# Second gather of a two-layer graph network: a list keyed by block pair and source half, 34 of its groups gathered beside the messages

## The reference

```python
# layer 0, a gated convolution over the edges
z = concat([x[src], x[dst], edge], 1) @ W.T + b
z = (z - mean(z, 0)) * rsqrt(var(z, 0) + 1e-5) * gamma + beta
msg = sigmoid(z[:, :128]) * softplus(z[:, 128:])
x1 = layernorm(x + x + zeros.at[src].add(msg))
# layer 1, on x1
mean1 = segment_sum(x1[src], dst) / max(count(dst), 1)
gain = tanh(norm(x1 - mean1))
h = x1 + 0.2 * (relu(x1 @ W1 + b1) @ W2 + b2) * gain
out = layernorm(x1 + layernorm(h) * gamma1 + beta1)
```

## Time and profile before

| what | us |
| --- | --- |
| median of 3 runs (4361.82 to 4364.86) | 4362.28 |
| the profiled execution, its own time | 4367.02 |
| its span | 4365.3 |
| busy: PE, DVE, ACT, POOL | 3008.4, 2770.6, 2254.1, 2572.3 |

### The profile page before, as it was taken

How to read it: one execution, slowest core, us unless ns; L and a number is a source line. 1 busy time by engine, 2 the same in 40 slices (tenths; PEclk the granted TensorE clock), 3 DMA queues, 4 the chain that set the end, 5 groups by cost and what they waited for, 6 DMA issues and landing times. The chain is left out here.

```text
span 4365.3 us, 81440 instructions
## 1 busy us (share of the span) xinstructions
PE 3008.4 (69%) x17430; PEld 2147.8 (49%) x17431; DVE 2770.6 (63%) x7511; ACT 2254.1 (52%) x6241; POOL 2572.3 (59%) x2618
## 2 busy tenths in 40 slices
PE   6865999899989999999998467666463333333330
PEld 2422444444447777777776366565343333333330
DVE  5798999899975555455554589888534334433337
ACT  2411898899866666666665799999310000000004
POOL 0687777777767777777776000000377777777770
PEclk8998999999999999999999788888665556566665
DMA  6333333333338888888888544443222222222241
GB/s 131 116 94 88 103 102 100 104 102 99 99 104 261 262 260 261 263 260 261 263 262 209 204 181 192 180 180 144 49 52 52 52 52 52 52 52 51 51 48 32
DMA packets 311358, 598.16 MB, mean 137 GB/s; under 512 B 53535, under 2 KB 191944, under 8 KB 305576
## 3 DMA queue, kind: packets, MB, share of 16 engines
q0 software_dynamic: 96992, 228.88, 20.9%
q1 hardware_dynamic: 175480, 246.10, 18.1%
q10 hardware_dynamic: 38736, 121.78, 7.4%
HBM read 406.57 MB, written 189.99 MB: 137 GB/s over the span
## 5 line engine op out<-in xcount | busy, mean ns | idle before, releaser
L346 POOL DMA_INDIRECT rec_d<-arena x830 | 873.0, 1052 | 375.3 <-issue 365.0
L1300 POOL DMA_INDIRECT arena<-x_tab,arena x880 | 847.3, 963 | 315.4 <-issue 277.3
L785 POOL DMA_INDIRECT arena<-b_tab,arena x880 | 838.6, 953 | 302.7 <-issue 262.1
L1332 PE MATMUL psum<-arena 128*128 128x129 f32 x1760 | 410.6, 426 | 694.9 <-DMA arena<-x_tab,arena 635.2
L1332 PEld LDWEIGHTS psum<-arena 128*128 128x128 f32 x1760 | 382.2, 329 | 723.6 <-issue 723.6
L1358 DVE TENSOR_TENSOR arena<-psum,arena 128x129 f32 x880 | 257.7, 293 | 673.3 <-PE psum L1332 553.7
L718 PE MATMUL psum<-arena 128*128 128x440 f16 x3360 | 664.8, 351 | 14.1 <-ACT arena L433 12.9
L806 DVE TENSOR_TENSOR arena<-psum,arena 128x512 f32<-128x512 f32 x440 | 283.6, 686 | 555.7 <-DMA arena<-b_tab,arena 323.2
L898 PE MATMUL psum<-weT,arena 128*128 128x256 f32 x1760 | 548.0, 393 | 58.0 <-DVE arena L806 55.2
L433 ACT ACTIVATE arena<-arena 128x128 f16<-128x128 f16 x1680 | 561.8, 386 | 0.0
L572 DVE TENSOR_SCALAR arena<-iota_t,arena 128x880 f16<-128x880 f16 x840 | 519.3, 663 | 48.4 <-PE psum L718 32.2
(11 more groups left out here) (207 smaller groups left out, 5226.3 us busy)
## 6 DMA issues: line engine op xcount, KB each, us to landing
z_d<-arena ACTq DMA_DIRECT2D x220, 512.0 KB
arena<-z_d SPq DMA_DIRECT2D x44, 2560.0 KB, 8.5
arena<-rec_d SPq DMA_DIRECT2D x220, 260.0 KB
arena<-in_edge_attr SPq DMA_DIRECT2D x83, 640.0 KB
arena<-b_tab,arena POOLq DMA_INDIRECT x880
arena<-x_tab,arena POOLq DMA_INDIRECT x880
rec_d<-arena POOLq DMA_INDIRECT x831, 2.0
b_tab<-arena ACTq DMA_DIRECT2D x49, 128.0 KB, 1.9
```

The lines of the kernel that those rows point to most:

```text
L346: nc.gpsimd.indirect_dma_start(rec_rows, bass.IndirectOffsetOnAxis(e_idx[:, s, k:k + 1], 0), e_buf[:, s, k, :], None).then_inc(s_es[s], 16)
L785: nc.gpsimd.indirect_dma_start(bg[:, s, k, :], None, b_tab, bass.IndirectOffsetOnAxis(rec[:, s, k, H:H + 1].bitcast(I32), 0)).then_inc(s_b ...
L1300: nc.gpsimd.indirect_dma_start(xg[:, s, k, :], None, x1_tab, bass.IndirectOffsetOnAxis(gi[:, s, k:k + 1], 0)).then_inc(s_xg[s], 16)
L1332: last = nc.tensor.matmul(bank(3 * s + q)[:, a * (H + 1):(a + 1) * (H + 1)], hotg[:, s, k, :], xg[:, s, k, :], start=True, stop=True)
```

## The change

- The `dst` list is keyed by 50 numbers in place of 49: the pair of destination blocks (`dst >> 8`, 25 pairs), plus 25 where the source is not in the first 16 blocks. Tiles whose sources all lie in the first 16 blocks come first. `l1_loc` now has 256 values.
- After 16 chunks of the messages DVE stops to normalise the 16 first blocks of `agg` (`normalise_early`), with a root by Newton steps in place of ACT's. SP stores them behind the rows of `x1_tab`. Two conditions on the counts (the first 16 blocks end at or before tile 300; the first 25 keys hold at least 272 tiles) are computed on the chip in `early_enough`; if one fails, POOL waits for the whole table. For the inputs of the reference the counts are 276 and 284, worked out from its edge list.
- POOL then gathers 34 groups of 8 tiles beside the messages and stores each to DRAM (`early_d`).
- The first normalisation moves into the block of the messages. DVE clears `agg1` in POOL's place.
- At the start of the messages SP writes zeros to all of `x1_tab`.
- In the second gather PE and DVE work in rounds of six groups, two early ones (SP loads them from `early_d`) and four gathered; then 8 gathered ones. Each tile has one-hots of 256 columns, two products and an add of 258 columns into a pair of blocks.

The diff, cut to its core:

```diff
-SLOTS = -(-((N_EDGES + BLOCKS * (P - 1)) // P) // (2 * G)) * (2 * G)
+SLOTS = -(-((N_EDGES + 2 * -(-BLOCKS // 2) * P) // P) // (2 * G)) * (2 * G)
+EARLY, EARLY_BLOCKS, EARLY_TILES = 34, 16, 300
+PAIRS = -(-BLOCKS // 2)
+KEYS = 2 * PAIRS
...
-                key(hi_d, dst_i)
+                after(nc.vector.tensor_scalar(t_int, dst_i, 8, None, ALU.logical_shift_right))
+                after(nc.vector.tensor_scalar(v_a, src_i, float(EARLY_BLOCKS * P), float(PAIRS), ALU.is_ge, ALU.mult))
+                after(nc.vector.tensor_tensor(hi_d, t_int, v_a, ALU.add))
...
+                def early_enough():
+                    after(nc.vector.tensor_scalar(early_key, tend[:, PAIRS - 1:PAIRS], float(G * EARLY), None, ALU.is_ge))
+                    after(nc.vector.tensor_tensor(early_src, early_src, early_key, ALU.mult))
+                    after(nc.vector.tensor_scalar(early_key, early_src, float(ROWS), None, ALU.mult))
+                    nc.vector.tensor_scalar(need[:], early_src, -32.0, 48.0, ALU.mult, ALU.add)
...
+        PAUSE = EARLY_TILES // (CG * YG) // CS + 1
...
+            @block.sync
+                def store_early():
+                    sp.wait_ge(s_blank, 16)
+                    sp.wait_ge(s_x1e, 1)
+                    sp.dma_start(x1_tab[ROWS:ROWS + EARLY_BLOCKS * P, :].rearrange("(b p) f -> p b f", p=P), x1e).then_inc(s_xs, 16)
+                sp.wait_ge(s_eps, 2)
+                sp.dma_start(x1_tab[0:ROWS, :].rearrange("(b p) f -> p b f", p=P), no_row.unsqueeze(1).broadcast_to([P, BLOCKS, H + 1])).then_inc(s_blank, 16)
-                chunks(sp, load)
+                chunks(sp, load, store_early, CS - 1)
...
+            @block.gpsimd
+                ready = nc.gpsimd.value_load(need[0:1, 0:1], min_val=16, max_val=48)
+                pool.wait_ge(s_xs, ready)
+                def keep(g):
+                    pool.wait_ge(s_xe[g % 2], (g // 2 + 1) * (16 * G))
+                    pool.dma_start(early_d[:, g, :], xe[:, g % 2, :, :].rearrange("p k f -> p (k f)")).then_inc(s_be[g % 2], 16)
+                for g in range(EARLY):
+                    if g >= 2:
+                        pool.wait_ge(s_be[g % 2], g // 2 * 16)
+                    for k in range(G):
+                        nc.gpsimd.indirect_dma_start(xe[:, g % 2, k, :], None, x1_tab,
+                                                     bass.IndirectOffsetOnAxis(l1_idx[:, g * G + k:g * G + k + 1], 0)).then_inc(s_xe[g % 2], 16)
+                    if g >= 1:
+                        keep(g - 1)
+                keep(EARLY - 1)
...
+                def normalise_early():
+                    dve.wait_ge(s_fl, EARLY_TILES // YG + 2)
+                    for b in range(EARLY_BLOCKS):
+                        last = nc.vector.bn_stats(six[:, b, :], agg[:, b, :])
+                    early(last)
+                    for b in range(EARLY_BLOCKS):
+                        last = nc.vector.bn_aggr(two[:, b, :], six[:, b, :])
+                    early(last)
+                    early(nc.vector.tensor_scalar(ve, two[:, :, 1:2].rearrange("p b a -> p (b a)"), LN_EPS, None, ALU.add))
+                    early(nc.vector.tensor_scalar(re.bitcast(I32), ve.bitcast(I32), 1, None, ALU.logical_shift_right))
+                    early(nc.vector.tensor_scalar(re.bitcast(I32), re.bitcast(I32), -1.0, float(0x5f3759df), ALU.mult, ALU.add))
+                    for _ in range(4):
+                        early(nc.vector.tensor_tensor(te, re, re, ALU.mult))
+                        early(nc.vector.tensor_tensor(te, te, ve, ALU.mult))
+                        early(nc.vector.tensor_scalar(te, te, -0.5, 1.5, ALU.mult, ALU.add))
+                        early(nc.vector.tensor_tensor(re, re, te, ALU.mult))
+                    nc.vector.memset(x1e[:, :, H:H + 1], 1.0)
+                    for b in range(EARLY_BLOCKS):
+                        last = nc.vector.tensor_scalar(x1e[:, b, 0:H], agg[:, b, :], two[:, b, 0:1], re[:, b:b + 1], ALU.subtract, ALU.mult)
+                    last.then_inc(s_x1e, 1)
-                chunks(dve, step)
+                chunks(dve, step, normalise_early)
...
+            def round_of(i):
+                order = (("early", 2 * i, 0, i + 1), ("direct", 4 * i, 0, 2 * i + 1), ("direct", 4 * i + 1, 1, 2 * i + 1),
+                         ("early", 2 * i + 1, 1, i + 1), ("direct", 4 * i + 2, 0, 2 * i + 2), ("direct", 4 * i + 3, 1, 2 * i + 2))
...
+                def product(u, place, kind, n, s, use):
+                    for k in range(G):
+                        wait(pe, s_fg, 8 * u + (k + 2 - RING))
+                        for h in range(2):
+                            last = nc.tensor.matmul(bank((8 * place + k) % RING)[:, h * (H + 1):(h + 1) * (H + 1)], hotg[:, place % 2, k, h * P:(h + 1) * P],
+                                                    rows[:, s, k, :], start=True, stop=True)
                         last.then_inc(s_sg, 1)
...
+                        last = nc.vector.tensor_scalar(hotg[:, place % 2, k, :], iota256[:], l1_loc[:, bass.ds(t, 1)], None, ALU.is_equal)
...
+                        dest = agg1.rearrange("p (c h) f -> p c (h f)", h=2)[:, bass.ds(pairs[k], 1), :].rearrange("p a f -> p (a f)")
+                        nc.vector.tensor_tensor(dest, bank((8 * place + k) % RING)[:, 0:2 * (H + 1)], dest, ALU.add).then_inc(s_fg, 1)
```

More of the change, by code:

```diff
@@ L479, in block_tiles @@
[L479 to L485 removed]
+                    n = offs.shape[1]
@@ L939, in build, with chunks @@
                              "message_transposed", "message_copied", "segment_product", "segment_added", "zero_weights"))
-        def chunks(eng, step):
+        PAUSE = EARLY_TILES // (CG * YG) // CS + 1
+        assert EARLY_TILES == (PAUSE * CS - 1) * CG * YG
+        def chunks(eng, step, pause=None, after_steps=0):
             for c in range(CS):
                 step(c, c, 0)
-            with eng.Fori(1, CHUNKS // CS) as it:
+            with eng.Fori(1, PAUSE) as it:
+                for j in range(CS):
+                    step(CS * it + j, j, it)
+            if pause is not None:
+                for j in range(after_steps):
+                    step(CS * PAUSE + j, j, PAUSE)
+                pause()
+                for j in range(after_steps, CS if after_steps else 0):
+                    step(CS * PAUSE + j, j, PAUSE)
+            with eng.Fori(PAUSE + (1 if after_steps else 0), CHUNKS // CS) as it:
                 for j in range(CS):
@@ L1091, in build @@
[L1091 to L1092 removed]
+        message_end = cursor[0]
+        fresh(27140)
         x1 = tmp([BLOCKS, H + 1], F32)
@@ new lines, in pair @@
+                def pair(c, j, it):
+                    first = isinstance(c, int) and c == 0
+                    for i in range(2):
+                        wait(act, s_zl[j + i], it * 16 + 16)
+                        u, v = chunk_half(j + i, 0), chunk_half(j + i, 1)
+                        nc.scalar.activation(u, u, ACT.Sigmoid, bias=bn_t[:, 0:1], scale=bn_s[:, 0:1]).then_inc(s_sig, 1)
+                        wait(act, s_spl, c + (i - 1))
+                        nc.scalar.activation(ex[:, i, :, :], v, ACT.Sigmoid, bias=stat[:, 5:6], scale=stat[:, 4:5]).then_inc(s_q, 1)
+                        if i == 0 and not first:
+                            copies(c - 2, (j - 2) % CS)
+                    for i in range(2):
+                        v = chunk_half(j + i, 1)
+                        wait(act, s_q, c + (i + 1))
+                        nc.scalar.activation(v, v, ACT.Identity, bias=bn_t[:, 1:2], scale=bn_s[:, 1:2]).then_inc(s_v, 1)
+                    for i in range(2):
+                        nc.scalar.activation(ex[:, i, :, :], ex[:, i, :, :], ACT.Ln, bias=stat[:, 6:7]).then_inc(s_lg, 1)
+                        if i == 0 and not first:
+                            copies(c - 1, (j - 1) % CS)
@@ L1197, in _ @@
+                for c in range(0, CS, 2):
+                    pair(c, c, 0)
+                with act.Fori(1, CHUNKS // CS) as it:
+                    for j in range(0, CS, 2):
+                        pair(CS * it + j, j, it)
+                for c in (CHUNKS - 2, CHUNKS - 1):
+                    copies(c, c % CS)
+                act.wait_ge(s_fl, CHUNKS * CG + 2)
+                act.wait_ge(s_eps, 2)
                 norm0.act_stats(0, agg, scr0)
@@ L1207, in _, with back, segment @@
             @block.tensor
             def _(pe):
+                def back(c, j, g):
+                    n, r = c * CG + g, ring(j, g)
+                    if g == 0:
+                        pe.wait_ge(s_msgT, c + 1)
+                    wait(pe, s_mc, n - 3)
+                    for k in range(YG):
+                        last = nc.tensor.transpose(bank(r)[:, k * P:(k + 1) * P], zl[:, j * CG + g, 0, k * P:(k + 1) * P], ident[:])
+                    last.then_inc(s_mt, 1)
+                def segment(c, j, g):
+                    n, r = c * CG + g, ring(j, g)
+                    _, window = nc.values_load_multi_w_load_instructions(
```

(23 more changed lines are left out.)

474 lines of the change are left out of this document (235 added, 239 removed).

## The result

The changed kernel takes **4247.5 us** (median of 4 runs, 4245.3 to 4253.9) where the kernel before, run beside it, takes 4362.6 (4361.8 to 4364.9): a ratio of 0.9738, 95% interval 0.9721 to 0.9755. The prediction was 4202, between 4080 and 4335, with 0.84 for faster. The profiled execution took 4249.4 us with a span of 4247.7, 117.6 less than the span before.

A forecast was written before the change was run, and what follows sets the result against it. POOL's gathers were taken to bound the second gather, with POOL idle in the messages. From the profiled 4367.0 us, +183 before that stage and -343 in it gave 4207, or 4202 us at the runs' median; range 4080 to 4335.

The forecast's parts named there:

- Term 1: Ranking of the list: 500 columns in place of 490 in each of 84 rounds, +4 us.
- Term 2: Start of the messages: SP's zeros for `x1_tab` delay the first z load, +19 us, bounds 0 and 21.
- Term 3: Messages: DVE feeds nobody for 12.6 us while normalising early, +12 us, bounds 5 and 13.
- Term 4: Early gathers: 18.6 us a group in the messages, 14.6 after; second gather begins at 3304, +183 us with earlier terms contained.
- Term 5: Second gather: 805 us in place of 1148, near POOL's 791, -343 us.
- it nearly fits: Early gathers: POOL not held by DVE, 14.6 us a group, 34 end at 3217; 4115 us, chance 10%.
- PE at the lower clock: Second gather: PE stays at its lower clock, the stage takes 893 us; 4290 us, chance 14%.
- one-hots shut POOL out: Messages: DVE's one-input one-hots also hold POOL, 27 us a group, second gather begins at 3400; 4298 us, chance 6%.
- the conditions fail: Early gathers: a count condition fails, POOL gathers the 34 groups behind the messages; 4550 us, chance 2%.
- stores' round trip: Early gathers: store landings of 8.5 us give 4354 us, no change; of 11 us, 4434; chance 13%.
- point of no gain: Early gathers: at 22 us a group the second gather's start has moved by all of the 343 us saved.
- The three things that I said would prove me wrong: Under 60 us between messages and second gather; a group there over 3 us from 14.6; PE without idle time in second gather.

The follow-up runs named there:

- e3: Changed kernel with the zeros for `x1_tab` stored behind the first four z loads, not ahead of them: 4228.7 us, ratio 0.9692.
- e2: Changed kernel with DVE waiting for PE's product once for two tiles in the second gather, not for each: 4217.1 us, ratio 0.9666.
- e11: Changed kernel with the second gather's one-hots 128 columns wide, used for both halves of a tile (half left out): 4205.0 us, ratio 0.9637.
- e4: Changed kernel with DVE's two-input product in each chunk of the messages replaced by two one-input instructions: 4223.2 us, one profiled run.
- e1: Changed kernel with each early group's store issued after the second gather of the next group, not after its eighth: 4162.5 us, ratio 0.9539.
- e12: Changed kernel with the edits of e1, e2 and e3, POOL's wait for its last stores moved to SP, and 32 early groups, not 34: 4097.3 us, ratio 0.9396.

## Why the prediction was right

**Term 1, the list (+4 us).** DVE's busy time up to 1293 us grew by 9 us (1111.2 for 1102.4), 3 of them in the scans and reductions over both lists, but the messages began where they did before. Too small to see: the start of the messages lies up to 6 us apart between kernels with the same stages ahead of it.

**Term 2, the blank table (+19).** 28.25 - 7.79 = 20.5 us, inside the bounds of 0 and 21, and e3 gave 19 back.

**Term 3, early normalisation (12.6 us, +12).** 12.5 us. The first early gather started at 2716.5 (forecast 2717) and the last add of the messages came at 3116 (forecast 3117).

**Term 4, the early groups (second gather at 3304, +183).** It began at 3293.6. 21 groups were stored by 3117, with 21.3 forecast, at 19.1 us each where I had 18.6. But that closeness is luck, errors that cancel. Of the 19.1 us, 10.2 are the gathers without their holds, 3.7 the holds, 0.6 the store's issue and 4.6 the wait for a landing; my 18.6 had 10.0, 4.0, 1.25 and 3.3 for them. The holds were 2.7 us a chunk (74.9 over 28 chunks, 46 held gathers) and not 3.7, because POOL often stood waiting for a store while DVE's second instruction ran, as at 2781.05. And six of the 21 stores landed behind a z load, in 8.4 to 10.4 us, where I took 3.6 for all (the sum has 3.3 for the messages and for the stretch behind them, though the text gives 3.6 and 3.0; with those it would be the same within 3 us). Behind the messages a group took 13.1 us, not 14.6: a store's issue costs 0.585 us and not the 1.25 that I took as the nearest row (0.67 less), the wait is 2.7 and not 3.3, and the first gather's gap of 0.3 lies in that wait. 13 groups x 1.5 = 20 us less; the 9.4 us from the last landing to the next stage, which no term had, took half of that back. So this term was too high by 10.

**Term 5, the second gather (805 us, -343).** It took 858 to 859: this is the term that was mis-sized, and the reason that the forecast lies 45 us under the result. POOL's 791 was not the bound; DVE's 7.32 us a group was, where I had 6.8. Eight one-hots take 2.44 us and not 2.16 (0.305 each; I had 0.27 from a row of 6272 columns), and eight adds from the first to the next one-hots 4.88 and not 4.64: 0.28 + 0.24 = 0.52 us, times 102 groups 53 us, the whole miss of this term; with the 10 of term 4 the other way it is the 45 of the result. The adds' part comes from the 0.22 us between two of them. I took 0.15 from the earlier trace rows, where only the first add of each PSUM bank waits for PE; in the changed kernel every add does. The row was right and its form wasn't the changed kernel's. e2 takes the 0.07 away and gets 33 us of the stage; e11 narrows the one-hots and gets 46. PE's clock of 0.86 was as forecast, with PE busy 614 of 858 us.

Of the rivals, *it nearly fits* fell by the 153 us that DVE sits idle ahead of the second gather; *PE at the lower clock* by the 0.86; *one-hots shut POOL out* by the 21 groups, and by e4, where one-input instructions far longer than those one-hots didn't shut POOL out; *the conditions fail* by gathers from 2716.5 on. The *stores' round trip* was there, in six of the 21 landings beside the messages and not in all; e1 prices the exposed landings, short and long, at 85 us. Its point of no gain, 22 us a group, was not reached: the average was (3281 - 2717) / 34 = 16.6.

The three things that I said would prove me wrong stayed away: the stretch between the stages is 180 us and not under 60, a group there is 1.5 us and not over 3 from 14.6, and PE's products have 225 us of idle time between them in the second gather.

## What to carry to other kernels

Work that is moved beside a busy stage pays for what the two share, and here half of the price, 85 of 172 us, was the wait for a store that could have been issued two gathers later. Put the store where its landing is covered. Then count how many pieces really fit, for each one beyond that is paid by all engines. When an engine's work for a piece doubles, price its waits by the form they will have, with every semaphore in them; 0.07 us an add was worth 30 us. A forecast that is right in its sum may hold errors that cancel, as the holds and the landings did; the views by line and by wait show them apart.

## What the runs showed of the hardware

- A store of 516 KB issued by POOL took its engine 0.585 us and landed in 3.0; issued 1.3 us after a load of 2560 KB on SP's queue, it landed in 9.3, 0.8 after that load. Its own packets were late: half of them started 8.0 us or more after the issue, with 1.8 for the middle one where no load was beside it.
- The stage in which POOL issues stores to the end went on for 12.4 us after the last issue with a wait for the landing, no bytes moving in the last 9.8, and for 9.8 us without it, no bytes in the last 7.2. A DRAIN of POOL fills the end: 8.96 and 9.56 us, and 7.86 in e12.
- DVE's adds came 0.22 us after one another where each also waited for PE, though the product was long done, and mostly 0.15 where only one in two or three did.
- One-input DVE instructions of 1.76 us slowed a gather by 0.43 to 0.63 us; those with two inputs held it to 0.83 us past their end.
- DVE itself was not held by POOL: of the 27 two-input instructions of L1222 beside early gathers the mean stayed 2.82 us, as before the gathers, though 13 began inside a gather, with up to 0.9 us of it to come (2778.12, the gather from 2777.29 to 2778.24); none of those took over 2.83. Two of them stood right behind DVE's instruction before, with 0.9 and 0.5 us of the gather to come (2720.34 and 3096.74), so no wait hides ahead of them. The Trainium skill (SBUF — State Buffer, on the shared port pair) has the later one wait for the whole instruction of the other; in this direction the trace doesn't agree.
